# Two wider first pieces, fold products behind the search and the routing, and one TensorE wait a step: a two-layer MoE and LoRA kernel on Trainium2

## What is computed

```python
def _L0_ffn_ref(x, Wg, bg, W1, W2):            # x: 4096 x 256 after the subject's matrix
    logits = flat_x @ Wg + bg                   # 4 experts
    top_vals, top_idx = jax.lax.top_k(logits, TOPK)
    ...
    for i in range(E):
        sel_p, sel_idx = jax.lax.top_k(score, capacity)      # 1,024 tokens
        h = jax.nn.gelu(flat_x[sel_idx] @ W1[i], approximate=False)
        out = out.at[sel_idx].add(h @ W2[i] * p)

def _L1_cond_ref(...):
    gate = _lora_linear(x, Wg, Ag, Bg, adapter_indices)
    up = _lora_linear(x, Wu, Au, Bu, adapter_indices)
    return _lora_linear(jax.nn.silu(gate) * up, Wd, Ad, Bd, adapter_indices)

x = x + _L0_ffn_ref(_L0_cond_ref(x, itok, L0_cond_weights), ...)
x = x + _L1_ffn_ref(_L1_cond_ref(x, ...), weight, scale_weight, bias)
```

## Time and profile before

| what | value |
|---|---|
| median of three runs | 626.85 us (625.8 to 627.24) |
| the profiled execution | 627.03 us, span 625.2 us |
| mean granted clock of PE | 0.972 of 2.4 GHz |
| busy: PE, DVE, ACT, POOL | 592.5, 357.5, 249.4, 130.3 us |
| instructions | 9902 |

### The profile page before, as it was taken

The page is one execution under the profiler, slowest core; times in us unless marked ns, Lnnn a source line. Parts: engine busy times, 40 slices in busy tenths (PEclk is TensorE's granted clock), DMA queues, the critical chain, the costliest instruction groups (busy, mean ns, idle before and its releaser), DMA issues.

```text
span 625.2 us, 9902 instructions
## 1 busy us (share of the span) xinstructions
PE 592.5 (95%) x3398; PEld 495.7 (79%) x3398; DVE 357.5 (57%) x794; ACT 249.4 (40%) x550; POOL 130.3 (21%) x111
## 2 busy tenths in 40 slices
PE   5768799999999999999999999999999999999994
PEld 2636699999999999977888888888888888888883
DVE  7887745775787566655445454454455444544533
ACT  2633235765874764654313422322334133223110
POOL 3000221554444461754003011030030020000000
PEclk9987669999999999999999999999999999999998
DMA  9998357425329321642004104032041040220012
GB/s 324 350 310 290 122 163 284 60 75 155 44 62 319 44 51 18 168 86 68 1 1 126 18 14 122 10 110 34 0 122 20 0 132 11 78 33 2 13 23 34
DMA packets 63932, 60.90 MB, mean 97 GB/s; under 512 B 37328, under 2 KB 56272, under 8 KB 62544
## 3 DMA queue, kind: packets, MB, share of 16 engines
q1 hardware_dynamic: 52880, 37.99, 20.2%
q0 software_dynamic: 8832, 22.09, 14.3%
q10 hardware_dynamic: 2176, 0.26, 0.3%
HBM read 45.05 MB, written 19.47 MB: 103 GB/s over the span
## 4 chain that ended last, share of the span: by engine, by line
PE 87%; DVE 9%; ACT 1%; DMA 1%; issue 1%; DVEq 0%; SPq 0%; ACTq 0%; POOLq 0%
PE bank L1193 24%; PE bank L1195 24%; PE bank L1194 23%; PE bank L1439 5%; PE bank L1406 2%; PE bank L1404 2%; DVE passed L846 2%; DVE mix_row L745 1%; PE bank L1250 1%; PE bank L1398 1%; PE bank L1302 1%; PE bank L1266 1%; PE bank L1293 1%; PE bank L1413 1%; PE bank L1414 1%
## 5 line engine op out<-in xcount | busy, mean ns | idle before, releaser
L689 ACT ACTIVATE act<-bank 128x512 f32<-128x512 f32 x64 | 38.4, 599 | 186.4 <-PE bank L1439 186.4
L1150 DVE TENSOR_TENSOR prod<-bank,act 128x512 f32<-128x512 f32 x64 | 44.2, 691 | 114.9 <-PE bank L1439 113.0
L1052 DVE TENSOR_TENSOR hid_lo<-hf,hid_hi 128x512 fp32r<-128x512 f32 (+1 forms) x72 | 45.6, 634 | 55.7 <-ACT hf L625 53.3
L1193 PE MATMUL bank<-w_hi,hid_hi 128*128 128x256 f32 x256 | 72.3, 282 | 0.3 <-DVE hid_lo L1052 0.3
L1194 PE MATMUL bank<-w_lo,hid_hi 128*128 128x256 f32 x256 | 71.7, 280 | 0.0
L1195 PE MATMUL bank<-w_hi,hid_lo 128*128 128x256 f32 x256 | 71.7, 280 | 0.0
L622 ACT ACTIVATE hid_hi<-bank 128x512 fp32r<-128x512 f32 (+1 forms) x72 | 39.8, 553 | 69.5 <-PE bank L1195 63.6
L450 POOL DMA_INDIRECT xg<-flat_rows,slot_row x32 | 33.8, 1057 | 134.1 <-DVE slot_row L912 84.3
L461 POOL DMA_INDIRECT x_rows<-y_sb,slot_row x32 | 51.8, 1617 | 43.9 <-ACT y_sb L590 33.0
L1193 PE MATMUL bank<-xs_hi,w_hi 128*128 128x512 f32 (+2 forms) x156 | 60.2, 386 | 0.2 <-ACT hf L625 0.2
L1195 PE MATMUL bank<-xs_hi,w_lo 128*128 128x512 f32 (+2 forms) x156 | 58.5, 375 | 0.0
(11 more groups left out here) (278 smaller groups left out, 1289.8 us busy)
## 6 DMA issues: line engine op xcount, KB each, us to landing
w_raw<-in_L_ffn_W SPq DMA_DIRECT2D x8, 1024.0 KB
flat_rows<-x_sb SPq DMA_DIRECT2D x8, 520.0 KB, 10.0
xT<-in_xT SPq DMA_DIRECT2D x8, 512.0 KB, 7.6
x_sb<-in_x SPq DMA_DIRECT2D x8, 512.0 KB, 8.6
outT<-out_sb SPq DMA_DIRECT2D x120, 32.0 KB
b_rows<-b_all_hi SPq DMA_DIRECT2D x1, 1152.0 KB
b_rows<-b_all_lo SPq DMA_DIRECT2D x1, 1152.0 KB
wdT<-in_wdT SPq DMA_DIRECT2D x1, 1024.0 KB, 5.9
```

The source lines that it names most:

```text
L689: act.activation(act1[h % 2][:, :], bank[h % 2][:, :], ACT.Silu).then_inc(silu1, 1)
L1052: dve.tensor_tensor(lo[:, n], hf[s % 2][:, n], hi[:, n].bitcast(f32), ALU.subtract).then_inc(hid0, 1)
L1150: dve.tensor_tensor(prod[h % 2][:, :], bank[2 + h % 2][:, :], act1[h % 2][:, :], ALU.mult).then_inc(prod1, 1)
L1193: pe.matmul(out, lh, rh, start=start, stop=False, skip_group_check=True)
```

## The change

On PE, the fold items are moved: none behind search steps 8 and 9 any more, two between marks and routing, three behind the routing. The eight filler products after the routing are gone (the two between the first transposes stay). The first block's steps 0 and 1 run in two pieces of 256 slots in place of four of 128, with the third transpose ahead of the first piece. In layer two the waits ahead of the gate products are removed, and the wait ahead of the down products asks for the product of the step before (`prod1` at s + 2, where s is two steps back) in place of the low part of two steps back; the last two steps keep the old wait. On ACT, the dummy Gelu that loads the table moves ahead of the fold copies.

```diff
-        WAIT_GATHER, WAIT_ROWS = 8, 2
+        WAIT_ROWS, FOLDS_FIRST = 2, 2
...
-            act.activation(warm[:, :], cols[:, 0:1], ACT.Gelu)
+                    act.activation(warm[:, :], cols[:, 0:1], ACT.Gelu)
...
                 last.then_inc(counted, 1)
-                for _ in range(2 if i < FOLD_STEP else 1):
-                    item(n)
-                    n += 1
+                if i < FOLD_STEP:
+                    for n in range(G - 2 * FOLD_STEP + 2 * i, G - 2 * FOLD_STEP + 2 * i + 2):
+                        item(n)
...
-            for n in range(n, ITEMS):
+            for n in range(G, G + FOLDS_FIRST):
                 item(n)
...
             route(0)
+            for n in range(G + FOLDS_FIRST, ITEMS):
+                item(n)
             pe.wait_ge(ident_in, 1)
             pe.wait_ge(hi0, KD)
             pe.wait_ge(item_ev, ITEMS)
-            keep_busy(WAIT_GATHER, bank[2], w1)
...
-            def first_up(c):
-
-                pe.wait_ge(xs_hi, c + 1)
-                pe.wait_ge(xs_lo, c + 1)
-                cs = slice(c * P, (c + 1) * P)
+            def first_up(j):
+
+                pe.wait_ge(xs_hi, 2 * j + 2)
+                pe.wait_ge(xs_lo, 2 * j + 2)
+                cs = slice(j * BT // 2, (j + 1) * BT // 2)
                 for h in range(2):
                     for k in range(KD):
                         last = product(bank[h][:, cs], at(w1, every, k, slice(h * P, (h + 1) * P)), at(xs[0], every, k, cs),
                                        start=k == 0, stop=k == KD - 1)
-                    if c == GB - 1:
+                    if j:
                         last.then_inc(up0, 1)
...
-            for c in range(2, GB):
-                first_up(c - 2)
-                first_transposed(c)
-            for c in range(2, GB):
-                first_up(c)
+            first_transposed(2)
+            first_up(0)
+            first_transposed(3)
+            first_up(1)
...
-            def down1_(s, h, t, par, first):
-                pe.wait_ge(hid1_s, s + 1)
+            def down1_(s, h, t, par, first, ends=False):
+
+                if ends:
+                    pe.wait_ge(hid1_s, s + 1)
+                else:
+                    pe.wait_ge(prod1, s + 2)
...
-                    if not (first and h < 2):
-                        pe.wait_ge(silu1, s - 1)
-                        pe.wait_ge(prod1, s - 1)
+                    if first and h == 2:
+                        pe.wait_ge(prod1, 1)
```

5 lines of the change are left out of this document (2 added, 3 removed).

## The result

The changed kernel took 620.0 us (median of 4 runs, 619.69 to 620.34), the kernel before 627.05 us beside it (4 runs, 625.8 to 627.37): a ratio of 0.9894, 95% interval 0.9875 to 0.9912. The prediction said 619.0, with 617.3 to 623.0 as its range. The changed kernel was timed a second time further down: 621.31 us.

A forecast was written before the change was run, and what follows sets the result against it. TensorE (PE), in the critical chain for 87% of the span, was taken as the bound. With the clock held, 6.0 + 2.1 = 8.1 us off 627.03 gave 618.9, rounded to 619; range 617.3 to 623.0.

The forecast's parts named there:

- the forecast's own: Range of the clock-held case alone, 617.3 to 620.3 us, around 618.9; that case had chance 0.50.
- rival (a): The clock is lost before piece 0, so the kernel takes 621.5 us; chance 0.31.
- a clock that holds through the first pieces: Forecast case: full clock kept through the first up steps, 8.1 us gained, 618.9 us; chance 0.50.
- the scan near 57.7: Sign at the search's end: the scan starts near 57.7 us instead of 59.22.
- the first transpose near 70.3: Sign behind the routing: first transpose near 70.3 us; at 72 or later, folds there run at half speed.
- Part 1, the search: Fold products leave search steps 8 and 9: DVE's work behind comes 1.55 us earlier; routing taken as late by 0.
- Part 2, three items behind the routing: Three fold items replace the eight fillers: 4.5 us at full level, first transpose loses 0.35 us; Gelu load move costs nothing.
- Part 3, two pieces: First up steps: 24 products fewer, 5.1 us less PE work; step 2 begins 6.0 or 4.2 us earlier.
- The exposed low part: Between fourth transpose and piece 1, PE waits about 1 us for a low part that other products hid before.
- Part 4, the clock: Behind step 2: gain 2.1 us if the clock holds, 1.35 if lost; five to three for holding.
- Part 5, layer two: Removed waits ahead of gate products gain 0; the new wait ahead of down products costs 0.
- Part 6, the second gather: Second block's gather lands 8.3 us after the fourth transpose, half a microsecond to spare; a miss costs about as much.

The follow-up runs named there:

- before once more: The kernel before, run again without any edit for a second trace: 625.46 us in one run.
- tighter version: The change plus a later wait for the last fold copy, fourth transposes inside piece 0, and a down-weight low part moved on DVE: 618.99 us, again 619.52.
- pieces alone: The kernel before with only the two pieces of 256 slots and their new call order; folds, fillers and waits as before: 622.01 us, ratio 0.9922.
- folds alone: The kernel before with the change's fold and Gelu-load placing and without the eight fillers, four narrow pieces kept: 620.09 us, ratio 0.9891.
- waits only: The kernel before with only the change's layer-two waits: 626.96 us, ratio 1.0007.
- all folds ahead: The change with all five fold items ahead of the routing and the eight fillers back behind it: 624.7 us, ratio 0.9965.
- search only: The kernel before with the two fold items moved out of the search to join the other three ahead of the routing: 628.16 us, ratio 1.0018.
- the change once more: The changed kernel timed again without any edit: 621.31 us, ratio 0.9909.
- no fillers: The change without its two filler products between the first and second block of transposes: 620.31 us, ratio 0.9887.
- both kernels with more fillers: The kernel before with twelve fillers behind the routing instead of eight, 622.47 us; all folds ahead with twenty instead of eight, 623.62 us.

## Why the prediction came out right, point by point

The time fell 1.0 us above the forecast and well inside the range. The second measurement, 621.31, is inside the range too, but outside the forecast's own (617.3 to 620.3) and next to rival (a). The mechanism that carried the forecast, a clock that holds through the first pieces, was the right one for the first profiled execution and not for the second. Two of its signs were given as times in the span, the scan near 57.7 and the first transpose near 70.3. They came at 59.16 and 71.95, both behind the late start of 1.50 us; without it they are 57.66 and 70.45. Its terms:

**Part 1, the search.** The gain of 1.55 us was there to a hundredth in the profiled pair (1.56). It was right for that pair and too large for the kernel. The kernel before once more lost only 0.11 in the same place, because the clock came back during the first fold item, and of five executions with these items in the search three lost 0.1 to 0.2. The term was read from one execution, and its size hung on a clock that moves between executions. Routing was late by nothing (7.18 us from the scan in both), as said.

**Part 2, three items behind the routing.** 0.56 us lost ahead of the first transpose, 0.35 predicted. The items took 4.59 us (66.69 to 71.28) where I had put 4.5, and the wait behind them was 0.68 where I had put 0.42. The tighter version shows that this loss hardly counts: with the first transpose back at the gather, the third one comes no earlier. The Gelu load cost nothing.

**Part 3, two pieces.** First transpose to step 2: 7.6 predicted with the clock held (70.25 to 77.85), 7.69 measured. With the clock lost: 9.45 predicted, 9.34 measured. The exposed low part: about 1 us predicted, 1.02 measured. What the text got wrong is which edit earns it. It counted the 24 products saved at the half-level price, 5.1 us. Once the clock holds, narrow products are 0.11 us apart as well, and the width is worth next to nothing: with fillers up to the gather, narrow pieces reach 8.00 us and wide ones 7.98, and moving the folds alone reached the change's time. The two edits are two ways to the same gain, and they don't add: the pieces alone won 4.6 us, the folds alone 6.5, both 7.05 in their first measurement and 5.35 in the second.

The rule of the Trainium skill that the prediction weighed, "TensorE: Matmul & The Clock Gate", section Back-to-back issue gap (distance is columns over clock), would have given pieces alone no gain. They won 4.6 us, so the trace's equal distances for 128 and 256 columns decide. The same section of the Trainium skill gives that rule for an isolated product. Of a stream it says that the loading of the weights sets the distance too, and of the rule's full-speed form that it counts narrow products too low. So it speaks against the cut less than the prediction has it.

**Part 4, the clock.** This was called open, five to three for holding, and it is open in the kernel itself: one profiled execution of the change held the clock, another lost it at piece 0. Between step 2 and the second block 1.96 us were won where it held, 2.1 predicted; where it was lost, 6.01 us in place of 7.60, so 1.59, where 1.35 was predicted. My reason for holding, dense work on both sides of the light stretch, is what the runs bear out for its first side, and as a tendency. With eight fillers and then 1.3 to 2.6 us of idle PE, none of six profiled executions kept the clock: five had it low at the first product (before, before once more, waits only, pieces only, all folds ahead), and one lost it at the fourth (search only). With work up to the last microsecond ahead of the first transpose, be it folds or fillers, the first product ran at full speed in all eight, and six held it into step 2 (the change, no fillers, the tighter one twice, and both kernels with more fillers). Two lost it, the change once more at its fourth product and folds only at its twentieth. That the idle time is the cause is shown twice by an edit of one number, eight fillers to twelve and eight to twenty. That its absence is enough is not shown, and the change once more is against it. Nor does the dense work on the far side of the light stretch decide alone: the change and the change once more have the same.

**Part 5, layer two.** Nothing, as predicted, and now measured alone. One reading was too wide: the rows begin at 290 us, and ahead of that one gate product did wait, at 285.76, for 0.54 us on the product. It is the wait that the change keeps for `first and h == 2`, and PE waits there still (0.44 us at 278.39).

**Part 6, the second gather.** In the change SP's load behind that gather started at 84.77, 8.54 us after the fourth transposes (8.3 predicted), and PE asked at 85.28, so 0.5 us were left, as predicted:

```profile
84.77 0.38 SPq L383 DMA_DIRECT2D w_raw<-in_L_ffn_W  x1
```

The kernel with twelve fillers waited 0.60 us there, about what the prediction had put for a miss, but not for its reason. It left the gather 9.25 us from the fourth transposes (77.00 to 86.25), more than the 9.05 in the change. The gather came late by itself: SP's load behind it started 10.25 us after the fourth transposes. The last of the four gathers was issued at about the same point as in the change (5.37 us after them, 5.33 in the change). Why it landed 1.7 us later stays open.

**The offsets.** The profiled pair holds two terms of noise of opposite sign: a start of the search 1.50 us later, and 1.04 us less in layer one. They are 0.09 and 0.42 between the change and before once more, and this pair gives the cleaner account: 4.82 us (12.51 to 7.69) and 1.19 (6.83 to 5.64) won, 0.43 lost ahead of the first transpose (5.61 against 5.18), 0.11 won in the search. That is 5.7 us, and their times differ by 625.46 - 619.69 = 5.77. The 0.09 lost and 0.42 won leave 0.2 us in places that no edit touches.

## What to carry to other kernels

Where PE must wait for a transfer before its dense work begins, try to give it work right up to the landing, real work if some can be moved there: four more dummy products were worth 4.2 us here, since 48 products behind them ran at full speed. Count a saving of products at the level at which they will run once the other edits are in, not at the level in the trace of before, or the same microseconds are counted twice. A stall whose length depends on when the clock returns must be read from two executions. A clock that was held in one profile is no promise for the next one. Before a shorter wait is counted as won, look for what the next instruction on the way waits for: here the third gather took back what the first transposes had gained.

## What was not expected of the hardware

**The clock falls in mid-stream.** It fell at the fourth product of piece 0 in the change once more, within dense products, and at the twentieth narrow product in the kernel with only the folds moved, although the products around it were no lighter than those ahead. The light stretch from the first transpose to piece 0 ended 0.5 us before the fall in the first case and 3.1 us before it in the second. It was no lighter where the clock was lost than where it was kept: PE was busy for 1.35 of 2.85 us in the change once more and for 1.40 of 2.83 in the change.

**A late start.** The first search count came between 28.9 and 32.1 us over the profiled runs, in kernels that are equal up to there. In the change it came 1.50 us later than before because PE's second wait for a load took 2.56 us and not 1.03.

**A stall that comes and goes.** At the end of layer one, ACT waited 1.66 us for a product in the trace of before and 0.32 us in that of the change. First before, then the change:

```profile
267.22 0.38 ACT L622 ACTIVATE hid_hi<-bank 128x256 fp32r<-128x256 f32 x1 [1.66 <-PE bank L1195]
```

```profile
259.52 0.38 ACT L622 ACTIVATE hid_hi<-bank 128x256 fp32r<-128x256 f32 x1 [0.32 <-PE bank L1195]
```

PE's wait of 0.33 us for `hid_lo` that goes with it is there in five of the 14 profiled executions and not in the others, both with and without the change; the change once more has it and the change has not. From the second block's transposes to layer two those two differ by 0.91 us, and its cause stays open.
